# Storing split expert weights to device memory and reading them back, with four more experts computed transposed

## The reference

```python
x = x + 0.5 * ffn(layernorm(x))
x = x + mamba(layernorm(x))
x = x + 0.5 * ffn(layernorm(x))

def ffn(x):                      # 8 experts, all of them for every token
    router_probs = softmax(x @ w_router)
    gate_weights = softmax(x @ w_gating / 0.1)
    h = silu(x @ w_gate[e]) * (x @ w_up[e])          # 128 -> 512, each e
    expert_out = h @ w_down[e]                       # 512 -> 128, each e
    cw = router_probs * gate_weights
    cw = cw / (sum(cw) + 1e-9)
    return sum over e of expert_out[e] * cw[e]

def mamba(x):                    # inner width 256, 16 states
    xs, z = split(x @ W_in)
    xc = silu(conv4(xs) + conv_b)
    dt = softplus((xc @ W_x)[:64] @ W_dt + b_dt)
    h_t = exp(dt * A) * h_(t-1) + dt * xc * B_t      # over 1024 tokens
    y = sum_n h_t * C_t + xc * D_param
    return (y * silu(z)) @ W_out
```

## Time and profile before

| | |
|---|---|
| median of 3 runs | 1242.97 us (1241.31 to 1243.07) |
| profiled execution, its own time | 1242.44 us |
| its span, first to last instruction | 1240.6 us |
| PE busy | 1233.1 us, 99% of the span |
| DVE busy | 1143.4 us, 92% |
| ACT busy | 1003.6 us, 81% |
| POOL busy | 446.4 us, 36% |
| granted TensorE clock | 1.0 throughout |
| moved by DMA | 184.84 MB, mean 149 GB/s |

### The profile page before, as it was taken

How to read it: one execution, slowest core, us unless ns; L and a number is a source line. 1 busy time by engine, 2 the same in 40 slices (tenths; PEclk the granted TensorE clock), 3 DMA queues, 4 the chain that set the end, 5 groups by cost and what they waited for, 6 DMA issues and landing times.

```text
span 1240.6 us, 20186 instructions
## 1 busy us (share of the span) xinstructions
PE 1233.1 (99%) x7072; PEld 1058.2 (85%) x7072; DVE 1143.4 (92%) x1368; ACT 1003.6 (81%) x2122; POOL 446.4 (36%) x571
## 2 busy tenths in 40 slices
PE   9999999999999999999999999999999999999999
PEld 7787788888888888888888888888888888887887
DVE  6958899999999999999999999997999999978877
ACT  7678789798898898988879898797988978846654
POOL 1021134445453463453434434452444344402000
PEclk9999999999999999999999999999999999999999
DMA  8412458888788997987889887986688979932322
GB/s 227 111 27 45 105 116 174 165 171 167 162 176 178 183 187 157 198 170 165 181 180 187 166 196 160 191 181 138 131 166 169 196 169 194 182 63 43 74 48 60
DMA packets 121015, 184.84 MB, mean 149 GB/s; under 512 B 11344, under 2 KB 38096, under 8 KB 120912
## 3 DMA queue, kind: packets, MB, share of 16 engines
q0 software_dynamic: 53568, 97.54, 45.0%
q1 hardware_dynamic: 67344, 86.00, 26.6%
HBM read 83.30 MB, written 2.69 MB: 69 GB/s over the span
## 4 chain that ended last, share of the span: by engine, by line
PE 93%; DVE 3%; ACT 2%; issue 1%; DMA 1%; SPq 0%; DVEq 0%; ACTq 0%
PE PS L1105 28%; PE PS L996 19%; PE PS L999 18%; PE PS L997 18%; PE PS L1101 2%; PE PS L1097 2%; PE PS L1099 2%; PE PS L1163 1%; PE PS L1148 1%; DVE HB L1345 1%; PE PS L1032 1%; DVE HL L1301 1%; PE PS L1040 1%; DMA YE<-CWD 1%; PE PS L1003 0%
## 5 line engine op out<-in xcount | busy, mean ns | idle before, releaser
L1105 PEld LDWEIGHTS PS<-WD,HB 128*128 128x128 f32 x3200 | 393.9, 191 | 22.1 <-issue 2.0
L1105 PE MATMUL PS<-WD,HB 128*128 128x128 f32 x3200 | 395.9, 275 | 0.0
L1345 DVE TENSOR_TENSOR HB<-PS,HB 128x1024 f32<-128x1024 f32 (+1 forms) x336 | 322.9, 962 | 72.5 <-PE PS L999 56.7
L1555 ACT ACTIVATE HB<-PS 128x512 f32<-128x512 f32 x512 | 294.9, 596 | 95.5 <-PE PS L999 93.5
L1733 POOL DMA_DIRECT2D Y<-HS x252 | 221.8, 954 | 317.6 <-DMA Y<-HS 151.7
L996 PE MATMUL PS<-XH,WG 128*128 128x512 f32 x509 | 219.7, 432 | 0.3 <-ACT HB L1555 0.2
L996 PE MATMUL PS<-XH,WU 128*128 128x512 f32 x512 | 204.4, 399 | 0.4 <-DVE HB L1345 0.4
L999 PE MATMUL PS<-XH,WU 128*128 128x512 f32 x512 | 201.2, 393 | 0.0
L999 PE MATMUL PS<-XH,WG 128*128 128x512 f32 x509 | 200.7, 394 | 0.1
L997 PE MATMUL PS<-XH,WU 128*128 128x512 f32 x512 | 200.4, 391 | 0.0
L997 PE MATMUL PS<-XH,WG 128*128 128x512 f32 x509 | 199.3, 392 | 0.0
(11 more groups left out here) (164 smaller groups left out, 1572.9 us busy)
## 6 DMA issues: line engine op xcount, KB each, us to landing
BCB<-BCD SPq DMA_DIRECT2D x128, 512.0 KB, 5.2
Y<-HS POOLq DMA_DIRECT2D x252, 256.0 KB, 6.0
XT<-YE POOLq DMA_DIRECT2D x99, 256.0 KB, 5.1
YE<-CWD SPq DMA_DIRECT2D x27, 256.0 KB, 4.5
AT<-YE POOLq DMA_DIRECT2D x21, 256.0 KB, 3.3
WD<-in_L_ffn_w_down_dram SPq DMA_DIRECT2D x8, 256.0 KB, 6.0
XT<-in_L_attn_x_dram SPq DMA_DIRECT2D x7, 256.0 KB, 5.8
out_dram<-XT SPq DMA_DIRECT2D x7, 256.0 KB, 5.4
```

Source lines behind the costliest of these rows:

```text
L1105: z = pe.matmul(part(g, j), HB[:, i % NH, j * P:(j + 1) * P], WD[:, e, c, :], start=c == 0 and j == 0, stop=c == FC - 1 and j == SUB - 1)
L1345: v.tensor_tensor(H, PS[:, NG + i % 2:NG + i % 2 + n, :], H, ALU.mult).then_inc(S["v_h"], 1)
L1555: a.activation(HB[:, i % NH, :], gate(i), ACT.Silu).then_inc(S["a_sil"], 1)
```

## The change

Four experts more are turned, 31 in all: expert 0 of position 1, and experts 5, 6 and 7 of position 13. The ring `WDS` grows from two pairs to three. Each of the 16 different pairs of down weights is split once, at its first use (`MADE`: 10 pairs in position 0, 6 in position 1), and SP stores it to device memory, `WDD` (step `wd_store`, 256 KB each). The other 46 uses (`READ`) have no `wd_hi` and `wd_lo`; SP reads the pair from `WDD` into the ring (step `wd_load`, 256 KB), planned four slots before its first product and kept in SP's order behind the row loads of the experts before. A ring place is free when its last product is done and, for a made pair, its store has landed. `HURRY` goes from 0 to 1: until the first scans begin, every call of `side()` advances `before` of the first tile.

```diff
-HURRY = 0
+HURRY = 1
-TURNS = {0: range(1, 6), 1: range(1, 8), 14: range(0, 8), 15: range(0, 7)}
+TURNS = {0: range(1, 6), 1: range(0, 8), 13: range(5, 8), 14: range(0, 8), 15: range(0, 7)}
+WEIGHTS_RING = 3
+PAIRS_TURNED = [i for i in TURNED_SLOTS if i % PAIR == 0]
+MADE = [i for i in PAIRS_TURNED if not any(k % SLOTS == i % SLOTS for k in PAIRS_TURNED if k < i)]
+READ = [i for i in PAIRS_TURNED if i not in MADE]
...
+    def weight_loads():
+
+        while reads and (asked[0] == len(TURNED) or TURNED[asked[0]] * FC + FC > reads[0] - SPLIT - PAIR - 2):
+            step("wd_load", reads.pop(0))
...
             m = nd + SPLIT
-            if m % PAIR == 0 and m in TURNED_SLOTS:
+            if m in MADE:
                 split_at[m] = split(m)
                 if m not in scalar_splits:
                     step("wd_lo", m, v=.4)
+                    step("wd_store", m)
             m -= 1
             if m in scalar_splits:
                 step("wd_lo", m, after=split_at[m], v=.35)
+                step("wd_store", m)
+            m = nd + SPLIT + PAIR
+            if m in READ:
+                reads.append(m)
             row_loads()
+            weight_loads()
...
-        WDS = sb("WDS", [P, 2, 2, PAIR, P], F32R)
+        WDS = sb("WDS", [P, WEIGHTS_RING, 2, PAIR, P], F32R)
+        WDD = nc.dram_tensor("WDD", [E, FC // PAIR, P, 2, PAIR, P], F32).ap()
...
         def wait_weights_free(eng, i):
 
-            n = TURNED_SLOTS[i]
-            if n >= 2 * PAIR:
-                eng.wait_ge(S["m_dn"], [k for k in TURNED_SLOTS if TURNED_SLOTS[k] == n - PAIR - 1][0] + 1)
+            n = pair(i) - WEIGHTS_RING
+            if n >= 0:
+                eng.wait_ge(S["m_dn"], PAIRS_TURNED[n] + PAIR)
+                if PAIRS_TURNED[n] in MADE:
+                    wait_weights_stored(eng, PAIRS_TURNED[n])
...
+                elif s[0] == "wd_store":
+                    i = s[1]
+                    wait_weights_high(wt, i)
+                    wt.wait_ge(S["v_wd"], MADE.index(i) + 1)
+                    r = pair(i) % WEIGHTS_RING
+                    sy.dma_start(WDD[i // FC % E, i % FC // PAIR], f32(WDS[:, r])).then_inc(S[f"c_ws{r}"], 16)
+                elif s[0] == "wd_load":
+                    i = s[1]
+                    wait_weights_free(wt, i)
+                    wait_weights_stored(wt, [k for k in MADE if k % SLOTS == i % SLOTS][0])
+                    r = pair(i) % WEIGHTS_RING
+                    sy.dma_start(f32(WDS[:, r]), WDD[i // FC % E, i % FC // PAIR]).then_inc(S[f"c_wl{r}"], 16)
...
-                        wait_weights_high(wt, first)
+                        if first in MADE:
+                            wait_weights_high(wt, first)
+                        else:
+                            wait_weights_read(wt, first)
```

More of the change, by code:

```diff
@@ L445, in row_loads @@
             asked[0] += 1
+    reads = []
+    def weight_loads():
+        while reads and (asked[0] == len(TURNED) or TURNED[asked[0]] * FC + FC > reads[0] - SPLIT - PAIR - 2):
+            step("wd_load", reads.pop(0))
     begun = {"before": 0, "scans": 0, "closing": 0}
@@ L747, in macaron_program @@
             S[n] = ctx.enter_context(nc.semaphore(n))
+        for r in range(WEIGHTS_RING):
+            S[f"c_ws{r}"] = ctx.enter_context(nc.semaphore(f"c_ws{r}"))
+            S[f"c_wl{r}"] = ctx.enter_context(nc.semaphore(f"c_wl{r}"))
         for b in range(BR):
@@ L826, in wait_weights_high @@
             by_scalar = i in scalar_splits
-            same = [k for k in TURNED_SLOTS if k <= i and k % PAIR == 0 and (k in scalar_splits) == by_scalar]
+            same = [k for k in MADE if k <= i and (k in scalar_splits) == by_scalar]
             eng.wait_ge(S["a_wd" if by_scalar else "v_wh"], len(same))
@@ L840, in wait_weights_free, with wait_weights_stored, wait_weights_read @@
         def wait_weights_free(eng, i):
-            n = TURNED_SLOTS[i]
-            if n >= 2 * PAIR:
-                eng.wait_ge(S["m_dn"], [k for k in TURNED_SLOTS if TURNED_SLOTS[k] == n - PAIR - 1][0] + 1)
+            n = pair(i) - WEIGHTS_RING
[3 more added lines that the diff above has]
+                    wait_weights_stored(eng, PAIRS_TURNED[n])
+        def wait_weights_stored(eng, i):
+            r = pair(i) % WEIGHTS_RING
+            eng.wait_ge(S[f"c_ws{r}"], 16 * sum(k <= i and pair(k) % WEIGHTS_RING == r for k in MADE))
+        def wait_weights_read(eng, i):
+            r = pair(i) % WEIGHTS_RING
+            eng.wait_ge(S[f"c_wl{r}"], 16 * sum(k <= i and pair(k) % WEIGHTS_RING == r for k in READ))
         def added(g):
@@ L1091, in _ @@
                     if g in TURNED:
-                        W = WDS[:, pair(i) % 2]
+                        W = WDS[:, pair(i) % WEIGHTS_RING]
                         first = i // PAIR * PAIR
                         high = HI[:, TURNED_SLOTS[i] % HI_RING, :]
-                        wait_weights_high(wt, first)
+                        if first in MADE:
+                            wait_weights_high(wt, first)
+                        else:
+                            wait_weights_read(wt, first)
                         wait_high(wt, i)
                         pe.matmul(turned(g), W[:, 0, c % PAIR, :], high, start=c == 0, stop=False)
-                        wt.wait_ge(S["v_wd"], pair(i) + 1)
+                        if first in MADE:
+                            wt.wait_ge(S["v_wd"], MADE.index(first) + 1)
                         pe.matmul(turned(g), W[:, 1, c % PAIR, :], high, start=False, stop=False)
@@ L1307, in _ @@
                     wt.wait_ge(S[f"c_wd{i // FC % E}"], 16)
-                    v.tensor_copy(WDS[:, pair(i) % 2, 0], WD[:, i // FC % E, c:c + PAIR, :]).then_inc(S["v_wh"], 1)
+                    v.tensor_copy(WDS[:, pair(i) % WEIGHTS_RING, 0], WD[:, i // FC % E, c:c + PAIR, :]).then_inc(S["v_wh"], 1)
                 elif k == "wd_lo":
@@ L1312, in _ @@
                     wait_weights_high(wt, i)
-                    v.tensor_tensor(WDS[:, pair(i) % 2, 1], WD[:, i // FC % E, c:c + PAIR, :], f32(WDS[:, pair(i) % 2, 0]),
+                    v.tensor_tensor(WDS[:, pair(i) % WEIGHTS_RING, 1], WD[:, i // FC % E, c:c + PAIR, :], f32(WDS[:, pair(i) % WEIGHTS_RING, 0]),
                                     ALU.subtract).then_inc(S["v_wd"], 1)
@@ L1571, in _ @@
                     wt.wait_ge(S[f"c_wd{i // FC % E}"], 16)
-                    a.activation(WDS[:, pair(i) % 2, 0], WD[:, i // FC % E, c:c + PAIR, :], ACT.Copy).then_inc(S["a_wd"], 1)
+                    a.activation(WDS[:, pair(i) % WEIGHTS_RING, 0], WD[:, i // FC % E, c:c + PAIR, :], ACT.Copy).then_inc(S["a_wd"], 1)
                 elif k == "acc" and s[1] in scalar_weighs:
```

2 lines of the change are left out of this document (added).

## The result

The changed kernel takes 1254.56 us (median of 4 runs, 1252.76 to 1257.27) against 1242.55 us for the kernel before: the ratio is 1.010, with a 95% interval of 1.0077 to 1.0123. It is 1.0% slower, 15 us above the forecast and 10 us above its range. The profiled execution took 1252.76 us, with a span of 1251.0, which is 10.4 us more than before. Three executions of these measurements stand apart with a much lower mean granted clock (one of the kernel before at 1760 us, clock 0.655, and two of late_14 at 1759 and 2069 us, 0.655 and 0.556); medians and ratios here leave them out.

A forecast was written before the change was run, and what follows sets the result against it. PE, busy 99% of the span, was taken as the bound. Terms -3.2 + 0.55 - 1.4 + 0.5 + 0.3 = -3.25 us gave 1239.7 us from a median of 1242.97; range 1236.5 to 1244.5.

The forecast's parts named there:

- position 1's term: Position 1: scans meeting turned slots, and expert 0's rows landing just when needed, cost +0.3 us, bounds 0 and 3.6.
- With the scans out of the way they fit: Position 13: with scans ended sooner, DVE has room for 12 more remainders at 0.68 us, 8 us more.
- HURRY: Position 1: earlier preparation fills DVE's idle 14.6 us; first scan at 135 to 145 us, last ends before 1085.
- Position 13: Turned slots take 2.08 us instead of 2.28; its own two transpositions cost 0.55 us together.
- the second rival: DVE becomes the bound in position 13, PE waits 1.2 us each time; five stops give 1245.7 us; chance 0.14.
- The rival's objection: Against DVE binding in position 13: scans may slip, their last result being first needed over 70 us later.
- The first rival: Reads or rows late behind position 1's broadcasts, 1.3 us a stop, plus position 0: +3.1, 1242.8 us; chance 0.21.
- Position 0's stores: Position 0: stores queued ahead of the combine rows delay them, +0.5 us, bounds 0 and 3.5.
- the relief of position 14 by reads: Position 14: without the splits DVE's backlog should not form, -1.4 us, bounds 0 and -1.4.
- reads hidden in positions 14 and 15: Reads planned four slots ahead, 8.3 us, against landings of 4 to 7 us, so they cost PE nothing.
- PE's work: 16 more turned slots save 3.2 us, position 13's transpositions cost 0.55: net -2.65 us on PE.

The follow-up runs named there:

- late_14: The full change with rows issued earlier and first broadcasts spread, but position 14's first three experts plain (28 turned): 1243.19 us, ratio 1.0000.
- rows_early: The full change with the planner's pause before transposing the combine weights removed (ROWS 4.0 to 0.0): 1250.49 us, ratio 1.0069.
- hurry0: The full change with HURRY back at 0, nothing else: 1255.12 us, ratio 1.0094.
- reads_only: The full change's stores, reads and ring of three, with the earlier kernel's 27 turned experts and HURRY 0: 1245.33 us, ratio 1.0024.
- split_anew: The kernel before with the 31 experts turned, weights split anew each time, ring of two, HURRY 0: 1257.10 us, ratio 1.0115.
- hurry_alone: The kernel before with HURRY 1 and nothing else: 1259.29 us, ratio 1.0129.
- no_exp0: The full change without turning expert 0 of position 1 (30 turned): 1259.15 us, ratio 1.0137.
- no_pos13: The full change without the three turned experts of position 13 (28 turned): 1251.69 us, ratio 1.0072.
- both_31: The full change, all 31 turned, with no pause before transposing the combine weights and the first broadcasts spread: 1250.57 us, ratio 1.0049.
- burst_spread: The full change with the first tile's three broadcasts issued one at a time between preparation steps: 1252.87 us, ratio 1.0085.
- stores_in_1: both_no_pos13, but position 0 stores nothing, position 1 splits anew and stores all 16 pairs, only positions 14 and 15 read: 1242.41 us, ratio 0.9993.
- both_no_pos13: The full change without position 13 (28 turned), no pause before transposing the combine weights, first broadcasts spread: 1242.51 us, ratio 1.0000.

## Why the prediction was wrong

**The step that failed** is position 1's term, "+0.3 for the others, bounds 0 and 3.6", into which the rows for expert 0 were put ("needed just when they land ... within the same 0.3"). DVE waited 4.2 us for them, and PE lost 2.4 + 0.6 + 1.6 (the last at the lower clock level) = 4.6 us; with the rows issued 6.4 us sooner position 1 took 4.9 us less (rows_early). The mistake was in how "just when they land" was read. The weighing stands in DVE's order ahead of the next products and remainders, so its lateness stops PE except for the little that PE has in hand: of DVE's 4.24 us of waiting 3.0 became stops. The row load's landing, 5 us, is not in the planner's order, and the forecast had that time in hand: the rows' 6.9 us in position 0 had already made PE wait. The stop at 92.9 (1.0 us) belongs to the same term: expert 0 turned a wait with slack into one without. So does the burst at 168 (1.5 us). The term was +0.3, with an upper bound of 3.6, and measured 4.6 + 1.0 + 1.5 = 7.1 us.

**The second step that failed** is "With the scans out of the way they fit", on which position 13 was put at no cost beyond its transpositions. The scans were not out of the way: their last instruction ended at 1129.5 us instead of before 1085, and the two stops in position 14 cost 4.7 us. The next two paragraphs take its halves, HURRY and position 13.

**HURRY** failed outright. The forecast had the first scans at 135 to 145 us and the last over before 1085; the first scan started at 169.6, the last scan instruction ended at 1129.5 and the last product at 1133.0. In the full change it brought little forward: SP issues the burst at 151.2 us with it and at 154.0 without it (hurry0, with a time the same within the intervals), against 140.9 in the kernel before. Expert 0's turning, with its own weighing, `HI` and `HL`, holds the preparation back further than HURRY moves it: with HURRY at 0 the burst is at 140.9 and 137.0 us without that expert (before, reads_only) and at 156.8 and 154.0 with it (split_anew, hurry0). And an earlier burst is not an earlier scan: in hurry_alone the first scan starts 6.5 us later than before. Where HURRY does bring the burst forward, the burst meets row loads and reads, and the loss is larger (hurry_alone 1.0129, no_exp0 1.0137). The forecast used the idle 14.6 us of DVE in position 1 as if the preparation's only price were DVE time; its other price is the transfers that it starts.

**Position 13** came out in two halves. PE's part was right: 12 slots at 2.08 us. Its 12 remainders fitted without a stop, so the second rival's place was wrong. Its mechanism was right one position later: the scans slipped past position 13 into 14. There a turned slot takes 2.08 us, and `h` and the remainder at their spacing of 0.60 us leave DVE 0.88, less than one scan product of 1.22. The rival's objection, "the scans may slip instead", was named as harmless and was the harm: 2.7 + 2.0 us. no_pos13 and late_14 show it from either side, and both_31 that it comes with position 13 alone, the scans having begun no later.

**The first rival** (reads or rows late behind the burst) had its place right, and for the full change its price. There it is 1.4 to 1.5 us at 168 (position 2 took 2.3 less in burst_spread), and where the burst comes early it is 3.1 us for one read, against 1.3 priced. What is queued behind the burst lands after 10.4 to 13.2 us, against a median of 5.1 for rows and 2.8 for reads. The Trainium skill ("DMA: Bandwidth & Descriptors", Queues, rings and completion order) has descriptors consumed in ring order on each DMA engine, by which what is queued behind the burst is late: the traces agree. It was priced as a rival to the forecast, though it is a loss that adds to others.

**Position 0's stores.** Position 0 took 1.0 us more against +0.5 forecast, within its bounds. The rows land at 40.06 instead of 38.5 us, DVE waits 1.98 instead of 1.1, and with the stores moved away position 0 takes 69.6 us (stores_in_1, which also orders the planner's work anew). But how much of it the stores cost is not shown: the three kernels that store nothing took 70.5, 70.8 and 71.2 us there (before, split_anew, hurry_alone), those that store 70.7 to 71.7, and three with the same order there (both_31, both_no_pos13, late_14) are 1.0 us apart.

**Right:** the counts; 2.28 and 2.08 us a slot; the relief of position 14 by reads, -0.8 to -1.1 us in no_pos13, reads_only, both_no_pos13 and stores_in_1 against -1.4; reads hidden in positions 14 and 15. The PE work saved is real and small, and most of the new stops are each nearly as large as all of it.

**The balance**, by terms: -3.2 + 0.55 (PE's work) - 1.0 (position 14's relief) + 1.0 (position 0) + 4.6 (rows of expert 0) + 1.0 (stop at 92.9) + 1.5 (burst) + 4.7 (scans in position 14) = +9.2 us. The span grew by 10.4; of the other 1.2, 0.7 is the later start and 0.5 positions 3 to 12. The median grew by 12.0, 1.7 more than the profiled run, which was the fastest of the four. Two of the four had a mean granted clock of 0.995 and 0.996, so longer stretches at the lower level; the stops behind them are not seen in a profile. Between the forecast of -3.25 and the +12.0 measured lie 15.3 us: 6.8 of position 1's term, 4.7 of the scans in position 14, 0.9 of the relief and of position 0, 1.2 of the later start and positions 3 to 12, and 1.7 by which the median is above the profiled run.

The forecast's range failed because position 1's term went past its own upper bound (7.1 against 3.6), and because the range took the bounds as alternatives: position 1, the second rival's stops and position 0 can come together, and did. That they share a cause, an order written by a planner that does not count the row load's landing or PE's wait for `HL`, is an argument from its code.

**Left open.** Whether position 13 pays without giving up 14, if the decays and the closing of the last tile are planned earlier; that wasn't tried. The spread of both_31 has no more than the argued explanation. What position 0's stores cost by themselves, and what the third ring place does alone, no run separates.

## What to carry to other kernels

When an order is written out by hand or by a planner, price a new consumer by when its inputs land, not by the work saved: a turned slot saved 0.2 us, and one weighing ahead of its rows cost 4.6. Moving a stream earlier moves its transfers too, so look for what stands behind its largest burst in the same queue. And slack that a slower form of the work left to another engine (2.28 us a slot for DVE against 2.08) is used by somebody: see who, before it is taken away, also in the next stretch.

## What the runs showed of the hardware that was not expected

- A stop of 2.2 us and one of 0.46 were followed by a stretch at the lower clock level: 0.43 us a matmul instead of 0.23, for six of them. hurry0 has the same pair at the same place, with 2.61 and 0.46 us of idle PE, and its matmuls go on at 0.23, at a granted clock of 1.00 from 106 to 112 us. In position 14 PE is idle for 2.55 us in both_31, 2.55 in hurry0 and 2.56 in the full change, and only in both_31 do slow starts follow (a clock of 0.50 from 1112 to 1114 us). So whether a stop costs this as well is not fixed by its length. The kernels without large stops have a mean clock of 1.000 in the profiled run, most of those with the longest 0.995 to 0.997 (but hurry0, with stops of 2.8 and 2.7 us, and rows_early, with 3.2 and 2.8, have 1.000).
- Three broadcasts of 512 KB on SP's queue make a transfer of 256 KB behind them land after 10.4 to 13.2 us, in seven kernels (9.6 in the kernel before; 8.6 in hurry0, whose row load is issued 4.8 us after the burst instead of 1.4 to 2.8). The same transfers alone take 2.8 us (weights) and 5.1 us (rows).
- 17 MB more of traffic, from 184.8 to 201.9 MB in the full change with its 46 reads, is no cost that could be measured as such outside position 0: both_no_pos13, with 40 reads, is at 1.0000.
